# The 64-key attentions give their context transposed: values and ones as 32-column weights

## What is computed

```python
def _attention(v_in, k_in, q_in, mask, Wv, Wk, Wq, Wo, bo):     # L1
    v, k, q = (einsum('nkhd,ed->nkhe', x.reshape(N, S, H, HD), W) for x, W in ...)
    energy = einsum('nqhd,nkhd->nhqk', q, k)
    energy = where(mask == 0, -1e20, energy)
    attn = softmax(energy / sqrt(E), axis=-1)
    out = einsum('nhql,nlhd->nqhd', attn, v).reshape(N, S, E)
    return out @ Wo.T + bo
...
x = ln(x + attention(x, x, x)); x = ln(x + attention(ctx, ctx, x))   # L1, both masked
x = x + mha(ln(x)); x = x + mha(ln(x), ln(tokens))                   # L3, not masked
```

## Time and profile before

| | us |
|---|---|
| median of 3 runs | 2005.97 |
| lowest, highest | 2002.24, 2006.39 |
| the profiled execution, device time | 2001.38 |
| its span | 1999.8 |

### The profile page before, as it was taken

One profiled execution on the slowest core, in us unless ns is written; L12 is line 12 of the kernel. 1 busy time (PEld: TensorE's weight loads), 2 busy tenths in 40 slices (PEclk: granted clock), 3 DMA queues, 4 the chain that ended last, 5 costly groups with the idle time before them and its releaser, 6 DMA issues. The chain is left out here.

```text
span 1999.8 us, 55013 instructions
## 1 busy us (share of the span) xinstructions
PE 1634.3 (82%) x17114; PEld 1295.9 (65%) x17114; DVE 1369.9 (69%) x4364; ACT 1171.9 (59%) x3299; POOL 942.3 (47%) x1373
## 2 busy tenths in 40 slices
PE   6999889898899677999999775449999885449882
PEld 6888778787787565777777562237777664337671
DVE  3778667676687556888777546868888774427673
ACT  2776657575666335777877432238888773127771
POOL 2354353334443345555666342444454444646773
PEclk8999999999999897999999796769999996559996
DMA  8766666565566003221000000000000000136765
GB/s 229 151 154 133 138 135 130 125 145 127 126 137 142 11 24 123 103 102 67 22 18 16 1 0 0 0 4 1 0 7 14 12 10 16 47 99 207 205 212 158
DMA packets 214845, 167.40 MB, mean 84 GB/s; under 512 B 27632, under 2 KB 188784, under 8 KB 214448
## 3 DMA queue, kind: packets, MB, share of 16 engines
q1 hardware_dynamic: 206128, 142.88, 28.6%
q0 software_dynamic: 8576, 22.88, 3.5%
HBM read 91.92 MB, written 73.76 MB: 83 GB/s over the span
## 5 line engine op out<-in xcount | busy, mean ns | idle before, releaser
L731 ACT ACTIVATE sb_probs<-sb_probs,sb_work 128x128 f32<-128x128 f32 x512 | 198.7, 406 | 168.0 <-DVE sb_work L636 168.0
L281 POOL TENSOR_SCALAR sb_next_var_eps<-sb_next_moments 128x1 f32<-128x1 f32 (+1 forms) x184 | 45.1, 245 | 468.0 <-DVE sb_next_moments L276 467.8
L883 POOL TENSOR_TENSOR sb_work<-sb_work,sb_cols 128x512 f32<-128x512 f32 x128 | 134.2, 1048 | 216.1 <-ACT sb_work L1100 134.5
L1026 DVE TENSOR_REDUCE sb_work<-PS 128x8 f32<-128x512 f32 x256 | 175.3, 685 | 46.2 <-PE PS L925 44.3
L1028 DVE TENSOR_TENSOR sb_work<-PS,sb_work 128x512 f32<-128x512 f32 x256 | 177.1, 692 | 8.8
L1060 ACT ACTIVATE sb_work<-sb_work 128x512 f32<-128x512 f32 x256 | 161.5, 631 | 32.9 <-DVE sb_work L1028 26.8
L899 PE MATMUL PS<-sb_ident,sb_work 128*128 128x128 f32 x1024 | 149.6, 286 | 15.4 <-ACT sb_work L1100 10.1
L952 PEld LDWEIGHTS PS<-sb_v_ones,sb_work 128*64 128x64 f32 x4096 | 132.2, 139 | 24.0 <-issue 15.5
L952 PE MATMUL PS<-sb_v_ones,sb_work 128*64 128x18 f32 x4096 | 144.1, 213 | 4.4 <-ACT sb_work L1066 3.0
L1066 ACT ACTIVATE sb_work<-PS 128x512 f32<-128x512 f32 x256 | 139.5, 595 | 9.3 <-PE PS L899 6.0
L899 PEld LDWEIGHTS PS<-sb_ident,sb_work 128*128 128x128 f32 x1024 | 113.4, 144 | 43.2 <-issue 31.2
(11 more groups left out here) (274 smaller groups left out, 4445.6 us busy)
## 6 DMA issues: line engine op xcount, KB each, us to landing
rel_scratch<-sb_work SPq DMA_DIRECT2D x64, 516.0 KB, 7.7
sb_work<-rel_scratch SPq DMA_DIRECT2D x64, 512.0 KB, 6.5
expert_rows<-sb_blank SPq DMA_DIRECT2D x36, 520.0 KB, 2.9
sb_w_up<-expert_halves SPq DMA_DIRECT2D x23, 512.0 KB, 3.8
sb_w_down<-expert_halves SPq DMA_DIRECT2D x23, 512.0 KB
expert_halves<-sb_e_halves POOLq DMA_DIRECT2D x16, 512.0 KB, 6.1
sb_work<-expert_rows SPq DMA_DIRECT2D x23, 260.0 KB, 3.3
sb_e_raw<-e_W POOLq DMA_DIRECT2D x16, 256.0 KB, 5.8
```

The source lines that it names most:

```text
L731: ins = e.activation(probs[:, j], probs[:, j], ACT.Exp, bias=neg_max[:, j:j + 1], scale=-1.0, accum_out=row_sum[:, j:j + 1])
L883: e.tensor_tensor(k_masked[:, u3], k_sb[:, u3].rearrange("p (b k) -> p b k", b=2).unsqueeze(2) .to_broadcast([P, 2, 4, S]), col("place").u ...
L1026: e.tensor_reduce(top, mine, AX.X, ALU.max).then_inc(sem("att_max_ready"), 1)
```

## The change

The product of probabilities and values is turned round. The values are now the weights: `v_wide` holds, for each group g of four heads and each pair p in it, the 8 + 8 value columns of the pair in a field of 48 columns with zeros between, so that 32 columns taken from column 16p hold the pair at its place p and zeros at the other. The transposed probabilities stream past, and the two pairs of a group are summed in PSUM. Each group writes its own 32 partitions, at `tile_position=(0, 32 * g)`: 32 columns of TensorE's array. `ones_wide` does the same with ones, for both sequences at once, so each of a head's 8 partitions receives the head's denominator for all 128 queries. What comes out has the features on the partitions and the tokens along the free axis: the transposed context and, beside it in bank 5, its denominators. VectorE takes the reciprocal of 128 numbers per partition instead of 16 and writes the product into `att_ctxT`. The transpose L931, its copy L1073, `att_ctx` and the semaphores of both are gone; the output product waits for `att_ctx_ready`, and the writer of `att_ctxT` for the output product two tiles back.

```diff
-        v_ones = sb("v_ones", [P, 4, 2, H, HD + 1])
+        v_wide = sb("v_wide", [P, 4, 2, 4, 3 * 2 * HD])
+        ones_wide = sb("ones_wide", [P, 3 * 2 * HD])
-        den_inv = carve((H,))
-        att_ctx = carve((2, H, HD))
+        den_inv = carve((P,))
...
-        values = PS[:, 5, 0:H * (HD + 1)].rearrange("p (h w) -> p h w", h=H)
+        values, dens = PS[:, 5, 0:P], PS[:, 5, P:2 * P]
...
-                if late:
-                    e.wait_ge(sem("att_ctx_ready"), n)
-                    wait_alone(e, sem("att_added"), n - 1)
-                    e.transpose(PS[:, 6, 2 * P:3 * P], att_ctx[:, 1 - u % 2], ident[:, :]).then_inc(sem("att_ctxT_done"), 1)
...
-                    for i in range(8):
-                        for b in range(2):
-                            ins = e.matmul(values[S * b:S * b + S, 2 * i:2 * i + 2], att_probsT[:, i, S * b:S * b + S],
-                                           v_ones[:, u, b, 2 * i:2 * i + 2], start=True, stop=True,
-                                           skip_group_check=True)
+                    for b in range(2):
+                        for p in range(2):
+                            for g in range(4):
+                                e.matmul(values[32 * g:32 * g + 32, S * b:S * b + S],
+                                         v_wide[:, u, b, g, 2 * HD * p:2 * HD * p + 32],
+                                         att_probsT[:, 2 * g + p, S * b:S * b + S], start=(p == 0), stop=(p == 1),
+                                         tile_position=(0, 32 * g), skip_group_check=True)
+                    for p in range(2):
+                        for g in range(4):
+                            ins = e.matmul(dens[32 * g:32 * g + 32], ones_wide[:, 2 * HD * p:2 * HD * p + 32],
+                                           att_probsT[:, 2 * g + p], start=(p == 0), stop=(p == 1),
+                                           tile_position=(0, 32 * g), skip_group_check=True)
...
                 if late:
-                    e.wait_ge(sem("att_ctxT_kept"), n)
+                    e.wait_ge(sem("att_ctx_ready"), n)
+                    wait_alone(e, sem("att_added"), n - 1)
                     e.matmul(PS[:, 6, 3 * P:4 * P], att_ctxT[:, 1 - u % 2], w_out[late["name"]][:, :], start=True, stop=True)\
...
-                    e.reciprocal(den_inv, values[:, :, HD]).then_inc(sem("att_den_ready"), 1)
+                    e.reciprocal(den_inv, dens).then_inc(sem("att_den_ready"), 1)
                     e.wait_ge(sem("att_den_ready"), n + 1)
-                    wait(e, sem("att_ctxT_done"), n - 1)
-                    e.tensor_tensor(att_ctx[:, u % 2], values[:, :, 0:HD], den_inv.unsqueeze(2).to_broadcast([P, H, HD]),
-                                    ALU.mult).then_inc(sem("att_ctx_ready"), 1)
+                    wait(e, sem("att_out_done"), n - 1)
+                    e.tensor_tensor(att_ctxT[:, u % 2], values, den_inv, ALU.mult).then_inc(sem("att_ctx_ready"), 1)
...
-                if late:
-                    e.wait_ge(sem("att_ctxT_done"), n)
-                    if head:
-                        e.wait_ge(sem("att_transposed"), n + 4)
-                    wait(e, sem("att_out_done"), n - 2)
-                    e.activation(att_ctxT[:, 1 - u % 2], PS[:, 6, 2 * P:3 * P], ACT.Copy).then_inc(sem("att_ctxT_kept"), 1)
...
-                        ins = e.activation(v_ones[r, w3].rearrange("p b (h two) w -> p (b h) two w", two=2)
-                                           [:, :, half, 0:HD],
-                                           PS[r, 7, 2 * P:4 * P].rearrange("p (n two w) -> p n two w", two=2, w=HD)
-                                           [:, :, half], ACT.Copy)
+                        ins = e.activation(v_wide[r, w3].rearrange("p b g c -> p (b g) c")
+                                           .rearrange("p n (k two w) -> p n k two w", two=2, w=HD)[:, :, 0:3:2, half],
+                                           PS[r, 7, 2 * P:4 * P].rearrange("p (n k two w) -> p n k two w", k=2, two=2, w=HD)
+                                           [:, :, :, half], ACT.Copy)
```

More of the change, by code:

```diff
@@ L978, in att_vector @@
             if base == 0:
[L980 to L986, removed]
+                e.memset(v_wide[:, :], 0.0).then_inc(sem("att_v_zeroed"), 1)
+                e.memset(ones_wide[:, :], 0.0).then_inc(sem("att_v_zeroed"), 1)
+                e.wait_ge(sem("att_v_zeroed"), 2)
+                for half in range(2):
+                    for p in range(2):
+                        at = 4 * HD * p + HD * half
+                        e.memset(ones_wide[S * half:S * half + S, at:at + HD], 1.0).then_inc(sem("att_v_zeroed"), 1)
+                e.wait_ge(sem("att_v_zeroed"), 6)
             else:
```

## The result

| | before | after |
|---|---|---|
| median, with the runs taken side by side, us | 2005.8 (2002.2 to 2006.4) | 2071.2 (2068.3 to 2078.7) |
| the profiled execution, us | 2001.4 | 2072.5 |

The ratio is 1.034, with a 95% interval of 1.032 to 1.036: slower, as forecast, but by 65 us and not by 106. The forecast of 2112 us is 41 us too high, and the median lies 1 us above the lower end of the range, 2070.

What follows compares the result with a forecast made beforehand. VectorE's list was taken to bound msa and sa, TensorE ca1, a TensorE-ScalarE round trip ca. 30.4 + 26 + 30.4 + 20.5 = 107 us on 2001.4 gave 2108.7, put down as 2112 against the median; range 2070 to 2138.

Steps and rivals of the forecast that it cites:

- What bounds the kernel: VectorE's instruction list paces msa and sa, TensorE ca1, a round trip between TensorE and ScalarE ca.
- The reciprocal's size: VectorE's reciprocal, widened from 16 to 128 numbers, was to take 1.20 us instead of 0.25, +0.95 a tile.
- the lower bound: VectorE's reciprocal some 0.90 us (+0.65), if a third of the 70 ns belonged to the strided PSUM read.
- The steps from there: Reciprocal's +0.95 us carried to 32 tiles per attention: msa +30.4, ca1 +26, sa +30.4, ca +20.5 us.
- The chain in ca1: Dependence loop through TensorE and VectorE in ca1: 1.97 + 2.66 + (0.28 + 0.95) + 0.29 = 6.15 us a tile against 5.34.
- the step's 0.31: In ca, VectorE's 0.31 us a tile wait for the output projection is swallowed: 5.65 - 0.31 + 0.95 = 6.29.
- TensorE's products: Four column tiles run side by side: context 0.47 us, sums 0.47, together 0.94 against 1.11 before; no cost.
- ScalarE and the queues: ScalarE's 0.28 us copy goes, the output product's new wait is already met, no DMA moves: zero.
- The clock: More TensorE idling may bring more stretches at 1.2 GHz: up to +10 us at the upper end, none in the sum.
- The ordinary rate: Rival: VectorE's reciprocal adds only +0.04 us, together -14 us, 1992 us, faster; chance 0.11.
- Balance: Rival: reciprocal of about 0.5 us, gain cancelled where it adds about 0.25 us, 2006 us, no difference; chance 0.04.
- Tiles in series: Rival: TensorE's column tiles do not run side by side, block 3.8 us, some +280 us, 2290 us; chance 0.04.

Runs made afterwards that it cites:

- e1_narrow: The changed kernel with the reciprocal taken of only the first 16 of 128 denominators per partition (work left out): 1986.4 us, ratio 0.994 to the kernel before.
- e2_before_wide: The kernel before with its reciprocal run over all 144 numbers of a tile's product instead of every ninth: 2081.8 us, ratio 1.041.
- e4_double_sums: The changed kernel with TensorE's products with ones for the denominators made twice: 2067.8 us, ratio 1.035 to the kernel before.
- The probe: The changed kernel plus a phase of VectorE reciprocals at 11 widths, 1 to 512, from SBUF and PSUM: fixed 157 ns plus 6.25 ns an element.
- e11_before_order: The kernel before with only ScalarE's copies of q and k moved ahead of the first half's exponential: 2009.3 us, ratio 1.005.

## Why the prediction was right in its sign and 41 us too high

*What bounds the kernel.* Right. The loss is what VectorE's list gains in length: e1_narrow takes it away by the width of the reciprocal alone, e2_before_wide brings it about in the old kernel, and e4_double_sums shows that TensorE is not the bound.

*The reciprocal's size.* Here the sum went wrong: +0.70 us, not +0.95. The 0.25 us in 128 tiles are 32 of the 36 us by which the profiled execution (2072.5) stays under the sum of 2108.7. I read "4 and 8 nearly the same, 16 much more" as blocks of eight, which makes 68 ns a block and 8.5 ns an element. What the rows carry is less: one of three points, a mean of unlike instructions, lay 25 ns low, and the slope between two points that differ by 8 elements was stretched over 112. The probe has 6.25 ns an element, 5.9 times the ordinary 1.06, from 4 elements on. The line from 4 to 16 taken as straight would have given (248 - 174) / 12 = 6.2 ns an element and +0.69; the row of 8 elements, which did not fit it, should have widened the range and not chosen the model. The Trainium skill's "repeat count of 8" for Reciprocal ("VectorE: DVE Perf Modes", the walkthrough of the 8-slice pipeline), read as eight cycles an element, does not agree with it, and neither does the other reading, one cycle an element. What I gave as the lower bound, +0.65 with a third of the step laid to the strided read, was near in size and wrong in its reason: the stride costs nothing. That term set the lower end of the range, so it is luck that the range just holds the result.

*The steps from there.* With +0.70 the same steps give 22 us in msa, 18 in ca1 (1.97 + 2.66 + 0.98 + 0.29 = 5.90; measured 5.88), 22 in sa and 12.5 in ca, 75 together or 2077, against 2072.5 of the profiled execution. The chain in ca1 is the step that was most at risk, and it is right to 0.02 us. In sa the tile is 0.09 shorter than that, in ca 0.20. The starts of VectorE's instructions in one turn of four tiles say where. In sa, 0.07 us is the wait for scores of before, swallowed (the list of waits has only 0.04 of it, since it leaves out the shortest gaps), and 0.03 a gap ahead of the normalisation. In ca, 0.14 of the 0.20 was never there to be kept: the 5.65 from which the step started has three tiles at a lower clock in it. From 5.51 on, the tile gains 0.70, loses 0.31 between VectorE's product and its residual sum, as the step said, and 0.05 in small gaps, which makes the 5.84. The pair in ca, before and after:

```profile
1594.69 0.29 DVE L1036 TENSOR_TENSOR sb_work<-PS,sb_work 128x128 f32<-128x128 f32 x1
1595.30 0.29 DVE L1042 TENSOR_TENSOR sb_X<-sb_X,PS 128x128 f32 x1 [0.31 <-PE PS L972]
```

```profile
1640.91 0.29 DVE L1043 TENSOR_TENSOR sb_work<-PS,sb_work 128x128 f32<-128x128 f32 x1
1641.12 0.28 DVE L1048 TENSOR_TENSOR sb_X<-sb_X,PS 128x128 f32 x1
```

That the step's 0.31 came out is luck in part: it was 7.2 us over 23 tiles, and 3.5 of the 7.2 are the waits of the three slow tiles.

*TensorE's products.* Right. The context takes 0.47 us, as forecast. Four column tiles do run at once, and by e4_double_sums a pass costs 27 ns, a quarter of a full one. The measured speedup of packing in the Trainium skill ("TensorE: Matmul & The Clock Gate", "Measured speedup vs the span model"), 2.38 for three tiles with 512 moving, is 79% of three; 79% of four would be an estimated 37 ns a pass. The trace with 128 moving shows no such loss: here four cost no more than one.

*ScalarE and the queues.* L1073's 0.28 us and the transpose were counted at nothing in the slow case and are worth next to nothing there (the 68 us beside the 70 above); in e1_narrow, where the reciprocal is short, ca gains 0.14 us a tile at full clock, some 4.5 us.

*The clock.* Wrong in direction. I had allowed up to 10 us for more time at 1.2 GHz, since TensorE idles more. It was the kernel before that lost time by it. In ca, one tile of before (VectorE in order of time), and the stretch around its start at a granted clock of 0.55 (columns as further below):

```profile
1543.12 0.29 DVE L1036 TENSOR_TENSOR sb_work<-PS,sb_work 128x128 f32<-128x128 f32 x1
1544.85 0.29 DVE L1042 TENSOR_TENSOR sb_X<-sb_X,PS 128x128 f32 x1 [1.45 <-PE PS L972]
...
1549.73 0.29 DVE L1036 TENSOR_TENSOR sb_work<-PS,sb_work 128x128 f32<-128x128 f32 x1
```

```profile
1541.80:1545.20 3.40, 3.00 (x16) 3.02 (x15) 1.83 (x5) 2.18 (x7) 1.05 (x1) 0.55 0.00 0
```

That tile takes 6.61 us from one L1036 to the next. Three such tiles, from 1543.1, 1566.3 and 1611.2, take 6.6 us each where the tile at the same place in the loop otherwise takes 5.49; they cost some 3 us together. The change has none of them in ca. TensorE's transposes of before and after (min/median/max ns of one):

```profile
L899 PE MATMUL PS<-sb_ident,sb_work x248: 272/273/422, 1501.0 to 1664.9; 128*128 128x128 f32 x124
```

```profile
L901 PE MATMUL PS<-sb_ident,sb_work x236: 272/273/330, 1560.3 to 1728.5; 128*128 128x128 f32 x118
```

The windows of ca say the same, here after, then e2_before_wide (PE, PEld, DVE, ACT, POOL busy us, granted clock, DMA):

```profile
1580.00:1715.00 135.00, 108.59 (x1960) 76.62 (x1949) 116.67 (x255) 98.19 (x233) 56.92 (x115) 1.00 0.04 12
```

```profile
1600.00:1730.00 130.00, 108.70 (x1475) 81.66 (x1483) 110.67 (x237) 95.33 (x239) 53.08 (x106) 0.97 0.04 11
```

With the old products and the long reciprocal the granted clock was 0.97 in ca (two tiles take 6.6 us where those at the same places in the loop take 5.97 and 5.71), with the new ones and TensorE busy for a smaller share (80% against 84%) it stayed at 1.00, as it did in ca in the others of this study with the new products. But e11_before_order, with the old ones, has 1.00 as well. So whether the new products hold the clock up stays open. The 0.14 us a tile that the clock put into the 5.65 of before are in either case a part of what ca lost less than forecast.

*The rivals.* The ordinary rate fell with the 0.948 us. Its -14 us for a short reciprocal is near the -12 of e1_narrow in sum, but by luck in its terms: it gave ca 0.34 us a tile, and at full clock ca gains 0.14. Balance was put at +0.25 us and is at about +0.12. Tiles in series fell.

## What to carry to other kernels

Ask of each rewrite how many elements it gives to the slowest operation in it, and take that operation's rate from a measurement of its own at two widths far apart: here a single wide one would have been worth the whole argument. Turning a product round to save a transpose can spread a short vector over the free axis, and the division by it grows eightfold. Where another engine can do it, what decides is not its time but what it stands ahead of in that engine's list: the same two activations made 1995, 2011, 2031 and 2067 us by the order of the work around them, and the order that gained 0.15 to 0.2 us a tile in msa and ca1 left sa 0.4 us a tile slower. And look at the spread behind a mean before a sum rests on it: here a mean of 178 ns hid two kinds of instruction, and a pace of 5.65 us three tiles at a lower clock.

## What the runs showed of the hardware

- VectorE's float32 reciprocal, one waiting for the other, takes 157 ns and 6.25 ns an element of the free axis from PSUM, from 4 to 512 elements, and 4 ns less from SBUF. Every ninth number of PSUM costs the same as 16 side by side (257 ns).
- In the attentions, where it starts before the instruction ahead of it has ended, 16 elements are recorded with 248 ns and 128 with 948.
- ScalarE's logarithm of 128 numbers from PSUM takes 260 ns and the exponential of it from SBUF 310, together 0.57 us against 0.95 for the reciprocal on VectorE.
- Four float32 products of 32 columns each run at once on TensorE: 27 ns a pass with 128 moving, against 117 for a full-array pass.
- Three stretches in which the granted clock fell (0.55 in the one shown) made three tiles of ca 6.6 us long instead of 5.5.
